# Graph attention on one core: one more gathered tile in 45 groups fetched row by row, from ScalarE's queue

## The chip, the cores and the metric

The kernel runs on one core of one Trainium2 chip. The metric is the device time of one launch in microseconds; of the kernel before, three runs were timed.

## The reference

The reference is a two-layer graph attention network over 3,125 nodes and 103,125 directed edges (self edges stand apart, one per node). Cut to what matters here, one layer is:

```python
xn = layernorm(x) * g + b
xp = xn + (xn @ Wpos + bpos + deg * Wdeg + bdeg)
q, k, v = xp @ Wq + bq, xp @ Wk + bk, xp @ Wv + bv      # 8 heads of 16
att = clip(sum(q[dst] * k[src], per head) / sqrt(16), -50, 50)
alpha = softmax of att over the edges of each dst
x = x + segment_sum(v[src] * alpha, dst) @ Wo + bo
x = x + gelu(layernorm(x) @ W1 + b1) @ W2 + b2
```

The edges are sorted by destination. `k[src]` and `v[src]` are rows of a table of 3,200 x 256 floats (1 KB a row) that the kernel writes to HBM once per layer; fetching the row of each edge's source is the gather that this case is about.

## The kernel before

**Tiles and groups.** The edges are cut into 806 tiles of 128; four tiles make a group, 202 groups a layer (the last one has two tiles). The first six groups are seams: tiles in which two destination blocks meet, which need two one-hot matrices. The edge loop runs over the groups of a layer, and each engine has its own copy of it, kept in step by semaphores.

**One group on each engine.** GpSimd gathers the group's rows of the table with one indirect DMA per tile (L857) into a ring of eight groups, `kvr`; before it starts group n it waits for `s_msg` of group n-8 (L854). ScalarE builds the transposed one-hot of group n+2 (`edge_spread`, L1327 to L1339: an Abs activation, L1335, and a Relu, L1339, both 128x512; a seam group has two such pairs), after the two Exp activations of group n (`edge_exp`, L1341 to L1348), which wait for VectorE. TensorE spreads the queries over the edges (L1135) and sums the messages per destination (L1148). VectorE multiplies keys and queries (`edge_prod`, L1728 to L1735), reduces, clips and guards them (L1740 to L1751), multiplies values by the weights (`edge_msg`, L1753 to L1761, which signals `s_msg`) and adds the sums to `agg` (L1769).

**Dense parts.** The 25 destination blocks are handled in nine chunks. As soon as a chunk's edges are summed, its dense parts (norm, attention output, two layer norms, Gelu, and in the first layer also the next layer's projections) are worked off in the slots of the edge loop that follow, at fixed offsets from the chunk's base slot: chunks 0 to 8 have their bases at slots 32, 56, 81, 105, 129, 154, 178, 195 and 203. On ScalarE (L1296 to L1325) a root stands at base+3 (L1172), Gelu at base+6 and base+7 (L1294, two activations each), and in the first layer a second root at base+10. Exp, Gelu and Sqrt need different activation tables, so that each of these slots has a table load before it and one back. The program order of ScalarE in a slot is `edge_exp(n)`, `edge_spread(n + 2)`, `dense_parts`.

**Rows fetched by SyncE.** In eight groups a layer, 25, 50, ..., 200 (`ROW_GROUPS`, L122), the group's last tile is not gathered by GpSimd. SyncE reads the source numbers of the tile into registers, six at a time (L748), and starts one DMA of 1 KB per row (L751), in the 22 slots that end four slots before the group. The rows land in `kv_rows`, which has two buffers; VectorE then takes this tile in an instruction of its own (L1734, L1758). The source numbers are loaded to one partition at the start (L672), ahead of the stores of the first layer's table (L681) on the same queue, for which GpSimd's first gather waits. SyncE also issues the loads of destination rows (`relT`, L664), the ordering of `q` and `x` by block (L688, L693), the second layer's table (L721) and the output.

Of the kernel before, what the change touches and what calls it, by code (L numbers as in the profile page):

```python
# [25 lines left out]
I32 = mybir.dt.int32  # L26
U32 = mybir.dt.uint32
U8 = mybir.dt.uint8
ALU = mybir.AluOpType
ACT = mybir.ActivationFunctionType  # L30
AX = mybir.AxisListType.X
ENG = mybir.EngineType

P = 128
N, D, H, L, FF = 3125, 128, 8, 2, 512
# [3 lines left out]
NP = BLOCKS * P  # L39
# [14 lines left out]
GROUPS = SEAM_GROUPS + MAIN_GROUPS  # L54
# [14 lines left out]
KV = 2 * D  # L69
# [12 lines left out]
NCH = len(CHUNKS)  # L82
# [30 lines left out]
KV_PAIRS = [(b, min(2, BLOCKS - b)) for b in range(0, BLOCKS, 2)]  # L113
# [8 lines left out]
ROW_GROUPS = [25 + 25 * i for i in range(8)]  # L122
# [2 lines left out]
ROW_TILE = G - 1  # L125


DVE_NORM, DVE_O, DVE_LN2, DVE_Y, DVE_LN1, DVE_QKV, DVE_SCORES, DVE_LOOP = 0, 2, 4, 9, 11, 13, 15, 17
PE_OUT, PE_O, PE_LN2, PE_FF, PE_Y, PE_LN1, PE_QKV = 1, 2, 5, 6, 8, 12, 13
ACT_OUT, ACT_STD2, ACT_LN2, ACT_FF, ACT_STD1, ACT_LN1, ACT_Q, ACT_LOOP = 1, 3, 5, 6, 10, 12, 15, 16  # L130
# [33 lines left out]
def step_of(n):  # L164

    return n // GROUPS, n % GROUPS
# [6 lines left out]

def by_rows(n):

    return n % GROUPS in ROW_GROUPS


def pool_gathers(n):
# [4 lines left out]
def row_turn(n):  # L184

    l, g = step_of(n)
    return l * len(ROW_GROUPS) + ROW_GROUPS.index(g)


def is_seam(n):  # L190
    return n % GROUPS < SEAM_GROUPS
# [102 lines left out]
def build(nc, x_in, src_flat, src_tiles, dst_tiles, dst_last, weights, out):  # L294
    with ExitStack() as ctx:
        def sb(name, shape, dt=F32):
            return ctx.enter_context(nc.sbuf_tensor(name, shape, dt))

        def sem(name):
            return ctx.enter_context(nc.semaphore(name))  # L300

        bank = [ctx.enter_context(nc.psum_tensor(f"bank{i}", [P, 512], F32)) for i in range(8)]

        kv_table = [nc.dram_tensor(f"kv_table{l}", [NP, KV], F32, kind="Internal").ap() for l in range(L)]
# [46 lines left out]
        apart = sb("apart", [P, G * P], BF16)  # L351
        kvr = sb("kvr", [P, RING, G, KV])
        kv_rows = sb("kv_rows", [P, 2, KV])
        row_src = sb("row_src", [1, len(ROW_GROUPS), P], I32)
        onehot = sb("onehot", [P, OH, G, P])
        onehotT = sb("onehotT", [P, OHT, G, P])
        prod = sb("prod", [P, G, D])
# [3 lines left out]
        msg = sb("msg", [P, 2, G, AGG])  # L361
# [6 lines left out]
        number = sb("number", [P, BLOCKS])  # L368
# [125 lines left out]
        s_first_table = sem("s_first_table")  # L494
# [24 lines left out]
        s_table = [sem(f"s_table{u}") for u in range(2)]  # L519
# [8 lines left out]
        s_apart = sem("s_apart")  # L528
        s_kv = [sem(f"s_kv{r}") for r in range(RING)]
        s_row_src = sem("s_row_src")  # L530
        s_kv_rows = [sem(f"s_kv_rows{u}") for u in range(2)]
        s_oh = sem("s_oh")
        s_ohT = sem("s_ohT")
# [7 lines left out]
        s_msg = sem("s_msg")  # L541
# [24 lines left out]
        def buffer(phase, c):  # L566

            return (phase * NCH + c) % 2

        def stored(phase, c):  # L570

            return 16 * sum(CHUNKS[k][1] for p in range(1, phase + 1) for k in range(NCH)
                            if buffer(p, k) == buffer(phase, c) and (p, k) <= (phase, c))
# [55 lines left out]
        def _(sp):  # L629
# [37 lines left out]
            rel_rows(1)  # L667

            sp.wait_ge(s_rows, 16 * 2 * SC)
            for i, g in enumerate(ROW_GROUPS):  # L670
                c, row = divmod(row_of(g, at_begin=True) + ROW_TILE, P)
                sp.dma_start(row_src[0:1, i, :], step_src[row:row + 1, c * P:(c + 1) * P]).then_inc(s_row_src, 16)  # L672

# [6 lines left out]
                    sp.wait_ge(*read(0, i, "kv"))  # L680
                sp.dma_start(table[:, b0:b0 + nb, :], kv_of(b0, nb)).then_inc(s_first_table, 16)  # L681

            sp.wait_ge(s_row_src, 16 * len(ROW_GROUPS))
            for c, (b0, nb) in enumerate(NAT):
                ranks = read_block_ranks(ENG.SP, b0, nb)
                sp.wait_ge(*read(0, c, "q"))
# [66 lines left out]
            for l in range(L):  # L753
                for s in range(SLOTS):
# [3 lines left out]
                    for i, g in enumerate(ROW_GROUPS):  # L758
                        part = s - (g - 3 - ROW_SLOTS)
# [409 lines left out]
        def _(act):  # L1169
# [157 lines left out]
            def edge_spread(n):  # L1327

                for h, m in enumerate(hots(n)):
                    r = 2 * h + n % GROUPS % 2 if is_seam(n) else m % BODY  # L1330
                    if m % BODY == 0:
                        act.wait_ge(s_relT[m // BODY % 2], 16 * (m // BODY // 2 + 1))
                    if m:
                        act.wait_ge(s_ohT, m)
                    act.activation(apart[:], relT[:, m // BODY % 2, r, :], ACT.Abs, bias=minus_p[:]).then_inc(s_apart, 1)  # L1335
                    act.wait_ge(s_apart, m + 1)
                    if m >= OHT:
                        act.wait_ge(s_qe, group_of(m - OHT) + 1)
                    act.activation(onehotT[:, m % OHT, :, :].rearrange("p j e -> p (j e)"), apart[:], ACT.Relu, bias=1.0, scale=-1.0).then_inc(s_ohT, 1)  # L1339

            def edge_exp(n):  # L1341

                act.wait_ge(s_attc, n + 1)
                t = gathers(n)
                act.activation(ex[:, 0:t * H], attc[:, n % 2, 0:t * H], ACT.Exp).then_inc(s_ex, 1)  # L1345
                if n >= 2:
                    act.wait_ge(s_agg_ps, n - 1)
                act.activation(msg[:, n % 2, 0:t, D:AGG], attc[:, n % 2, 0:t * H].rearrange("p (j h) -> p j h", h=H), ACT.Exp).then_inc(s_den, 1)  # L1348
# [5 lines left out]
            for l in range(L):  # L1354
                for s in range(SLOTS):
                    n = l * GROUPS + s
                    if s < GROUPS:
                        edge_exp(n)
                        if s + 2 < GROUPS:
                            edge_spread(n + 2)  # L1360
                    dense_parts(l + 1, s)
                    if l + 1 < L and s - BASE[-1] in ACT_NEXT:
                        edge_spread((l + 1) * GROUPS + ACT_NEXT.index(s - BASE[-1]))

        @program.vector
        def _(dve):
# [193 lines left out]
            def by_head(t):  # L1560
                return t.rearrange("p b (h d) -> p b h d", d=HD)
# [164 lines left out]
            def edge_prod(n):  # L1726

                dve.wait_ge(s_kv[n % RING], landed(n))  # L1728
                dve.wait_ge(s_qe, n + 1)
                t = pool_gathers(n)  # L1730
                if by_rows(n):
                    k = row_turn(n)
                    dve.wait_ge(s_kv_rows[k % 2], 16 * P * (k // 2 + 1))
                    dve.tensor_tensor(prod[:, t, :], kv_rows[:, k % 2, 0:D], bank[2][:, t * D:(t + 1) * D], ALU.mult)  # L1734
                dve.tensor_tensor(prod[:, 0:t, :], kvr[:, n % RING, 0:t, 0:D], bank[2][:, 0:t * D].rearrange("p (j c) -> p j c", c=D), ALU.mult).then_inc(s_prod, 1)  # L1735

            def edge_att(n):
# [15 lines left out]
            def edge_msg(n):  # L1753

                dve.wait_ge(s_ex, n + 1)
                t = pool_gathers(n)
                if by_rows(n):
                    dve.tensor_tensor(by_head(msg[:, n % 2, t:t + 1, 0:D]), by_head(kv_rows[:, row_turn(n) % 2:row_turn(n) % 2 + 1, D:KV]),  # L1758
                                      ex[:, t * H:(t + 1) * H].rearrange("p (j h) -> p j h", h=H).unsqueeze(3).broadcast_to([P, 1, H, HD]), ALU.mult)
                dve.tensor_tensor(by_head(msg[:, n % 2, 0:t, 0:D]), by_head(kvr[:, n % RING, 0:t, D:KV]),  # L1760
                                  ex[:, 0:t * H].rearrange("p (j h) -> p j h", h=H).unsqueeze(3).broadcast_to([P, t, H, HD]), ALU.mult).then_inc(s_msg, 1)  # L1761
# [68 lines left out]
            for l in range(L):  # L1830
                if l:
                    dve.wait_ge(s_agg0, l * NCH)
                for s in range(SLOTS):
                    n = l * GROUPS + s
# [54 lines left out]
```

## Time and profile before

| | us |
|---|---|
| median of 3 runs | 2166.88 |
| lowest, highest | 2166.07, 2170.96 |
| the profiled execution | 2163.2 |
| its span | 2161.5 |
| POOL (GpSimd) busy | 1552.6 (72%) |
| DVE (VectorE) busy | 1713.3 (79%) |
| PE (TensorE) busy | 1429.3 (66%) |
| ACT (ScalarE) busy | 940.6 (44%) |
| granted TensorE clock, mean | 0.804 of full speed |

How to read it: the span is the time from the first to the last instruction of one profiled execution, and the 1.7 us around it belong to that execution's own time. Busy time counts compute instructions and GpSimd's indirect DMAs; register instructions and the DMA issues of SyncE are not counted. In the rows, PE, DVE, ACT, POOL and SP are TensorE, VectorE, ScalarE, GpSimd and SyncE; a q behind the name means the engine's sequencer.

### The profile page before, as it was taken

How to read it: one execution, taken by the hardware profiler on the slowest of the kernel's cores; microseconds unless marked ns; L12 is line 12 of the kernel's file. 1: busy time of each engine (PE TensorE's matmuls, PEld its weight loads, DVE VectorE, ACT ScalarE, POOL GpSimd, SP SyncE). 2: the span in 40 equal slices, each digit the busy share in tenths (PEclk: the TensorE clock that was granted, in tenths of full speed). 3: DMA queues.
4: the chain of work that ended last, by engine and by line, in shares of the span. 5: the costliest groups of instructions: out<-in, count | busy, mean ns of one | idle time of the engine just before them, and what ended most of it. 6: DMA issues, size and time to landing. Idle time of an engine off the chain costs nothing.

```text
span 2161.5 us, 38930 instructions
## 1 busy us (share of the span) xinstructions
PE 1429.3 (66%) x8227; PEld 1248.0 (58%) x8227; DVE 1713.3 (79%) x5135; ACT 940.6 (44%) x2179; POOL 1552.6 (72%) x1653
## 2 busy tenths in 40 slices
PE   4866676776667666666777656566666767665666
PEld 4655565655556555555656556565565656555565
DVE  8759888889888878787877777787777778777876
ACT  8333354444535353534454335344343535344344
POOL 6177777777777777777727777777777777777773
PEclk9979878777977788887888778877886778788788
DMA  2365544454444444444424444444444444444441
GB/s 88 111 185 157 161 150 150 143 151 135 139 141 127 143 136 143 128 143 136 133 69 145 126 136 136 140 126 140 136 136 129 139 136 130 137 136 139 127 140 58
DMA packets 127140, 289.73 MB, mean 134 GB/s; under 512 B 33572, under 2 KB 61152, under 8 KB 126912
## 3 DMA queue, kind: packets, MB, share of 16 engines
q0 software_dynamic: 77056, 210.21, 33.8%
q1 hardware_dynamic: 49856, 77.03, 10.8%
q8 instruction: 76, 1.25, 0.2%
q14 instruction: 152, 1.25, 0.2%
HBM read 275.44 MB, written 8.38 MB: 131 GB/s over the span
## 4 chain that ended last, share of the span: by engine, by line
POOL 40%; issue 20%; DVE 14%; PE 13%; ACT 5%; DMA 4%; SPq 3%; DVEq 1%; ACTq 0%
POOL kvr L857 40%; PE bank L1135 5%; PE bank L1148 4%; DVE agg L1769 4%; DMA kvr<-kv_table,srcidx 3%; DVE kvr L1378 2%; DVE prod L1735 1%; ACT apart L1335 1%; ACT onehotT L1339 1%; SPq L751 1%; DVE onehot L1723 1%; PE bank L1092 1%; ACT L1294 1%; ACT L1345 1%; SPq L748 1%
## 5 line engine op out<-in xcount | busy, mean ns | idle before, releaser
L857 POOL DMA_INDIRECT kvr<-kv_table,srcidx x1596 | 1512.8, 948 | 543.8 <-issue 476.6
L1135 PE MATMUL bank<-q,onehotT 128*128 x3320 | 612.6, 342 | 683.9 <-DVE prod L1735 407.5
L1135 PEld LDWEIGHTS bank<-q,onehotT 128*128 128x128 f32 x3320 | 521.9, 240 | 796.3 <-issue 795.1
L1148 PE MATMUL bank<-msg,onehot 128*128 128x136 f32 x3320 | 615.0, 345 | 1.4 <-DVE msg L1760 1.2
L1148 PEld LDWEIGHTS bank<-msg,onehot 128*128 128x128 f32 x3320 | 574.8, 253 | 3.7 <-DVE msg L1760 3.5
L1345 ACT ACTIVATE bank<-attc 128x32 f32<-128x32 f32 x404 | 81.2, 201 | 1118.4 <-DVE attc L1751 1114.2
L1769 DVE TENSOR_TENSOR agg<-agg,bank 128x136 f32 x1624 | 470.7, 290 | 66.2 <-PE bank L1148 59.4
L1735 DVE TENSOR_TENSOR prod<-kvr,bank 128x512 f32<-128x512 f32 (+1 forms) x404 | 273.7, 678 | 232.2 <-DMA kvr<-kv_table,srcidx 190.9
L1335 ACT ACTIVATE apart<-relT,minus_p 128x512 bf16<-128x512 bf16 x416 | 293.8, 706 | 7.1 <-DMA relT<-rel_table 6.7
L1723 DVE TENSOR_TENSOR onehot<-bank,rel 128x512 f32<-128x512 f32 x416 | 282.8, 682 | 0.2
L1760 DVE TENSOR_TENSOR msg<-kvr,bank 128x512 f32<-128x512 f32 (+1 forms) x404 | 272.1, 674 | 12.2 <-ACT bank L1345 11.9
L1740 DVE TENSOR_REDUCE att<-prod 128x32 f32<-128x512 f32 x404 | 273.3, 677 | 0.1
L1339 ACT ACTIVATE onehotT<-apart 128x512 f32<-128x512 bf16 x416 | 261.9, 629 | 13.2
L1348 ACT ACTIVATE msg<-attc 128x32 f32<-128x32 f32 x404 | 86.0, 213 | 0.0
L1746 DVE TENSOR_SCALAR attc<-att 128x32 f32<-128x32 f32 x404 | 80.4, 199 | 0.0
L1751 DVE COPY_PREDICATED attc<-attnan,zeros 128x32 f32<-128x32 uint8 x404 | 76.8, 190 | 0.0
L1745 DVE TENSOR_TENSOR attnan<-att 128x32 uint8<-128x32 f32 x404 | 74.8, 185 | 0.1
L1604 DVE TENSOR_TENSOR x<-x,bank 128x384 f32<-128x384 f32 (+1 forms) x36 | 18.9, 524 | 68.6 <-PE bank L1092 38.9
L1345 ACT ACT_TABLE_LOAD x51 | 65.4, 1283 | 0.9
L1092 PE MATMUL bank<-w,hT 128*128 128x128 f32 x400 | 59.4, 293 | 0.0
L1378 DVE TENSOR_TENSOR kvr<-kvr,q 128x3328 bf16<-128x3328 bf16 (+1 forms) x32 | 55.0, 1772 | 2.5 <-PE bank L884 2.4
L1079 PE MATMUL bank<-xnT,w 128*128 128x384 f32 (+1 forms) x144 | 55.4, 516 | 0.7 <-ACT xnT L1272 0.7
(219 smaller groups left out, 857.6 us busy)
## 6 DMA issues: line engine op xcount, KB each, us to landing
relT<-rel_table SPq DMA_DIRECT2D x104, 512.0 KB
kv_rows<-kv_table SPq DMA_DIRECT2D x2048, 1.0 KB
kvr<-kv_table,srcidx POOLq DMA_INDIRECT x1596
loop_kv<-kv_table SPq DMA_DIRECT2D x25, 128.0 KB, 2.8
kv_table<-qkv SPq DMA_DIRECT2D x25, 128.0 KB, 2.5
kv_table<-onehot SPq DMA_DIRECT2D x8, 256.0 KB, 2.2
w<-weights SPq DMA_DIRECT2D x2, 840.0 KB, 7.3
loops<-x_in SPq DMA_DIRECT2D x5, 320.0 KB, 5.4
```

The lines of the kernel that those rows point to most:

```text
L857: pool.indirect_dma_start(kvr[:, n % RING, j, :], None, kv_table[l], bass.IndirectOffsetOnAxis(ap=srcidx[:, step:step + 1], axis=0)).then_ ...
L1135: mm = pe.matmul(bank[2][:, j * D:(j + 1) * D], onehotT[:, m % OHT, j, :], q[:, bass.ds(ranks[j + h], 1), :].rearrange("p a c -> p (a c)") ...
L1148: mm = pe.matmul(sum_ps(n, k), onehot[:, m % OH, j, :], msg[:, n % 2, j, :], start=(m, j) == of[0], stop=(m, j) == of[-1])
L1335: act.activation(apart[:], relT[:, m // BODY % 2, r, :], ACT.Abs, bias=minus_p[:]).then_inc(s_apart, 1)
L1339: act.activation(onehotT[:, m % OHT, :, :].rearrange("p j e -> p (j e)"), apart[:], ACT.Relu, bias=1.0, scale=-1.0).then_inc(s_ohT, 1)
L1345: act.activation(ex[:, 0:t * H], attc[:, n % 2, 0:t * H], ACT.Exp).then_inc(s_ex, 1)
L1378: return dve.tensor_tensor(oh[:, k % 2, :, :, :], digit[:, 0:count_of, :].unsqueeze(1).broadcast_to(shape), of_step.unsqueeze(2).broadcast ...
L1723: dve.tensor_tensor(onehot[:, m % OH, :, :], iota_ps.unsqueeze(1).broadcast_to([P, G, P]), rel[:, row:row + G].unsqueeze(2).broadcast_to([ ...
L1735: dve.tensor_tensor(prod[:, 0:t, :], kvr[:, n % RING, 0:t, 0:D], bank[2][:, 0:t * D].rearrange("p (j c) -> p j c", c=D), ALU.mult).then_in ...
L1740: dve.tensor_reduce(att[:, n % 2, 0:t * H], prod[:, 0:t, :].rearrange("p j (h d) -> p (j h) d", d=HD), AX, ALU.add).then_inc(s_att, 1)
L1760: dve.tensor_tensor(by_head(msg[:, n % 2, 0:t, 0:D]), by_head(kvr[:, n % RING, 0:t, D:KV]), ex[:, 0:t * H].rearrange("p (j h) -> p j h", h ...
L1769: dve.tensor_tensor(target, target, sum_ps(n, j), ALU.add).then_inc(s_agg, 1)
```

## The change

Four more groups a layer, 46, 91, 136 and 181 (`ACT_ROW_GROUPS`), have their last tile fetched row by row. ScalarE does this: three rows a slot, right behind `edge_spread` and ahead of the dense parts, in the 43 slots that end four slots before the group. Each slot holds one register load of three values and three DMAs with a register address (the last one two). The rows have a buffer pair and semaphores of their own. SyncE loads four more rows of source numbers at the start. GpSimd gathers three tiles instead of four in these groups, and VectorE takes the fourth from the new buffers. The diff, cut to its core:

```diff
+ACT_ROW_GROUPS = [46 + 45 * i for i in range(4)]
+ACT_ROWS_A_SLOT = 3
+ACT_ROW_SLOTS = -(-P // ACT_ROWS_A_SLOT)
...
 def by_rows(n):
-    return n % GROUPS in ROW_GROUPS
+    return n % GROUPS in ROW_GROUPS + ACT_ROW_GROUPS
...
-            for i, g in enumerate(ROW_GROUPS):
+            for i, g in enumerate(ROW_GROUPS + ACT_ROW_GROUPS):
                 c, row = divmod(row_of(g, at_begin=True) + ROW_TILE, P)
                 sp.dma_start(row_src[0:1, i, :], step_src[row:row + 1, c * P:(c + 1) * P]).then_inc(s_row_src, 16)
...
+            def fetch_rows(l, i, part):                      # ScalarE
+                k = l * len(ACT_ROW_GROUPS) + i
+                if part == 0:
+                    if k == 0:
+                        act.wait_ge(s_row_src, 16 * len(ROW_GROUPS + ACT_ROW_GROUPS))
+                    if i == 0 and l == 0:
+                        act.wait_ge(s_first_table, 16 * len(KV_PAIRS))
+                    elif i == 0:
+                        for u in range(2):
+                            c = NCH - 1 - u
+                            act.wait_ge(s_table[buffer(l, c)], stored(l, c))
+                    if k >= 2:
+                        act.wait_ge(s_msg, (k - 2) // len(ACT_ROW_GROUPS) * GROUPS + ACT_ROW_GROUPS[(k - 2) % len(ACT_ROW_GROUPS)] + 1)
+                p0, p1 = part * ACT_ROWS_A_SLOT, min(P, (part + 1) * ACT_ROWS_A_SLOT)
+                nodes = nc.values_load_multi_w_load_instructions(row_src[0:1, len(ROW_GROUPS) + i, p0:p1], engines=(ENG.Activation,), min_val=0, max_val=NP - 1,
+                                                                 skip_runtime_bounds_check_because="the number of a node")[1]
+                for p, node in zip(range(p0, p1), nodes):
+                    act.dma_start(act_kv_rows[p:p + 1, k % 2, :], kv_table[l][bass.ds(node, 1), :]).then_inc(s_act_kv_rows[k % 2], 16)
...
                         edge_exp(n)
                         if s + 2 < GROUPS:
                             edge_spread(n + 2)
+                        for i, g in enumerate(ACT_ROW_GROUPS):
+                            part = s - (g - 3 - ACT_ROW_SLOTS)
+                            if 0 <= part < ACT_ROW_SLOTS:
+                                fetch_rows(l, i, part)
                     dense_parts(l + 1, s)
...
                 if by_rows(n):                               # VectorE, edge_prod; edge_msg alike
                     k = row_turn(n)
-                    dve.wait_ge(s_kv_rows[k % 2], 16 * P * (k // 2 + 1))
-                    dve.tensor_tensor(prod[:, t, :], kv_rows[:, k % 2, 0:D], bank[2][:, t * D:(t + 1) * D], ALU.mult)
+                    landed_rows, rows = (s_act_kv_rows, act_kv_rows) if n % GROUPS in ACT_ROW_GROUPS else (s_kv_rows, kv_rows)
+                    dve.wait_ge(landed_rows[k % 2], 16 * P * (k // 2 + 1))
+                    dve.tensor_tensor(prod[:, t, :], rows[:, k % 2, 0:D], bank[2][:, t * D:(t + 1) * D], ALU.mult)
```

## Rows read from the trace of the kernel before

**Rows 1.** The page, the chain that ended last, by engine

```profile
POOL 40%; issue 20%; DVE 14%; PE 13%; ACT 5%; DMA 4%; SPq 3%; DVEq 1%; ACTq 0%
```

**Rows 2.** Waits of POOL, whole run: us in total, times, longest us

```profile
POOL kvr L857 <- issue: 476.6, 1564, 0.3
POOL kvr L857 <- DMA kv_table<-qkv: 35.0, 1, 35.0
...
POOL kvr L857 <- DVE msg L1760: 9.1, 30, 0.3
```

**Rows 3.** Timeline, DVE and POOL: start us, us, engine, line, operation, tiles

```profile
153.20 0.68 DVE L1760 TENSOR_TENSOR msg<-kvr,bank 128x512 f32<-128x512 f32 x1
154.42 0.95 POOL L857 DMA_INDIRECT kvr<-kv_table,srcidx  x1 [0.30 <-issue]
...
481.27 0.68 DVE L1760 TENSOR_TENSOR msg<-kvr,bank 128x512 f32<-128x512 f32 x1
...
496.97 0.95 POOL L857 DMA_INDIRECT kvr<-kv_table,srcidx  x1 [0.30 <-issue]
```

**Rows 4.** Waits of DVE for gathers: whole run, then 607 to 1136, 1136 to 2162

```profile
DVE prod L1735 <- DMA kvr<-kv_table,srcidx: 190.9, 144, 3.9
...
DVE prod L1735 <- DMA kvr<-kv_table,srcidx: 36.1, 26, 3.4
...
DVE prod L1735 <- DMA kvr<-kv_table,srcidx: 154.8, 118, 3.9
```

**Rows 5.** SP's row DMAs and a three-value load (ns min/median/max), and a timeline row

```profile
L751 SPq DMA_DIRECT2D kv_rows<-kv_table x2048: 224/228/344, 139.2 to 2110.7; - x187
...
L623 SPq TENSOR_LOAD <-permrow x27: 280/928/947, 228.2 to 2147.0; - x27
...
241.92 2.32 SPq L751 DMA_DIRECT2D kv_rows<-kv_table  x6
```

**Rows 6.** DVE's register load, 704 to 705 us, and the timeline of DVE there

```profile
L618 DVEq TENSOR_LOAD <-rankrow x1: 342/342/342, 704.7 to 704.7; - x1
...
704.69 0.61 DVE L1623 SCALAR_TENSOR_TENSOR qkv<-u_deg,deg,bank 128x384 f32<-128x384 f32 x1 [0.52 <-PE bank L1046]
```

**Rows 7.** Timeline of ACT, a quick plain slot

```profile
168.91 0.20 ACT L1345 ACTIVATE bank<-attc 128x32 f32<-128x32 f32 x1 [2.36 <-DVE attc L1751]
...
169.90 0.63 ACT L1339 ACTIVATE onehotT<-apart 128x512 f32<-128x512 bf16 x1
172.45 0.20 ACT L1345 ACTIVATE bank<-attc 128x32 f32<-128x32 f32 x1 [1.92 <-DVE attc L1751]
```

**Rows 8.** Timeline of ACT and DVE, chunk 0: second Gelu slot, first root, second root

```profile
311.27 0.20 ACT L1345 ACTIVATE bank<-attc 128x32 f32<-128x32 f32 x1 [0.33 <-DVE attc L1751]
...
312.26 0.63 ACT L1339 ACTIVATE onehotT<-apart 128x512 f32<-128x512 bf16 x1
312.91 1.28 ACT L1294 ACT_TABLE_LOAD   x1
...
316.57 0.20 ACT L1345 ACTIVATE bank<-attc 128x32 f32<-128x32 f32 x1
...
316.80 0.69 DVE L1760 TENSOR_TENSOR msg<-kvr,bank 128x512 f32<-128x512 f32 x1
...
294.80 0.30 ACT L1172 ACTIVATE std<-mv,eps 128x3 f32<-128x3 f32 x1
...
296.11 0.17 DVE L1580 RECIPROCAL rstd<-std 128x3 f32<-128x3 f32 x1
...
330.08 0.30 ACT L1172 ACTIVATE std<-mv,eps 128x3 f32<-128x3 f32 x1
...
330.56 0.17 DVE L1580 RECIPROCAL rstd<-std 128x3 f32<-128x3 f32 x1
```

**Rows 9.** SP at the start: timeline row, and its waits

```profile
77.73 5.41 SPq L672 DMA_DIRECT2D row_src<-q  x8
...
SPq L681 <- DVE kvr L1537: 5.0, 4, 1.3
```

More of the change, by code:

```diff
@@ L186, in row_turn @@
     l, g = step_of(n)
-    return l * len(ROW_GROUPS) + ROW_GROUPS.index(g)
+    groups = ROW_GROUPS if g in ROW_GROUPS else ACT_ROW_GROUPS
+    return l * len(groups) + groups.index(g)
 def is_seam(n):
@@ L353, in build @@
         kv_rows = sb("kv_rows", [P, 2, KV])
-        row_src = sb("row_src", [1, len(ROW_GROUPS), P], I32)
+        row_src = sb("row_src", [1, len(ROW_GROUPS) + len(ACT_ROW_GROUPS), P], I32)
+        act_kv_rows = sb("act_kv_rows", [P, 2, KV])
         onehot = sb("onehot", [P, OH, G, P])
@@ L530, in build @@
         s_row_src = sem("s_row_src")
+        s_act_kv_rows = [sem(f"s_act_kv_rows{u}") for u in range(2)]
         s_kv_rows = [sem(f"s_kv_rows{u}") for u in range(2)]
@@ L681, in _ @@
                 sp.dma_start(table[:, b0:b0 + nb, :], kv_of(b0, nb)).then_inc(s_first_table, 16)
-            sp.wait_ge(s_row_src, 16 * len(ROW_GROUPS))
+            sp.wait_ge(s_row_src, 16 * len(ROW_GROUPS + ACT_ROW_GROUPS))
             for c, (b0, nb) in enumerate(NAT):
@@ L1757, in edge_msg @@
                 if by_rows(n):
-                    dve.tensor_tensor(by_head(msg[:, n % 2, t:t + 1, 0:D]), by_head(kv_rows[:, row_turn(n) % 2:row_turn(n) % 2 + 1, D:KV]),
+                    rows = act_kv_rows if n % GROUPS in ACT_ROW_GROUPS else kv_rows
+                    dve.tensor_tensor(by_head(msg[:, n % 2, t:t + 1, 0:D]), by_head(rows[:, row_turn(n) % 2:row_turn(n) % 2 + 1, D:KV]),
                                       ex[:, t * H:(t + 1) * H].rearrange("p (j h) -> p j h", h=H).unsqueeze(3).broadcast_to([P, 1, H, HD]), ALU.mult)
```

## Prediction

> **What bounds the kernel now.** I read the page's chain first. Six tenths of the chain that ended last are GpSimd's gathers with the issue gaps between them [rows 1]. One gather takes 0.95 us and the next starts 0.30 us later, so the cadence is 1.25 us [rows 3]. The waits of GpSimd come next [rows 2]: 1,564 of its 1,596 idle gaps before a gather are this issue gap, at most 0.3 us long. Besides them it waited 35.0 us for the second layer's table, and the 30 waits put down to VectorE's message together make 9.1 us, 0.3 us each, which is the issue gap again. So GpSimd runs without a stop inside both layers, and 1,596 x 1.25 = 1,995 us of the 2,161.5 us span are its cadence.
>
> Two reserves decide whether a shorter gather stream shows. **The ring**: gathers of group n wait for the message of group n-8. The message of group 3 ends at 153.20+0.68 = 153.88, and group 11's first gather starts at 154.42: 0.54 us to spare. At group 80 it is 496.97 against 481.95: 15.0 us [rows 3]. **VectorE's slack**: it waited for gathered rows 190.9 us in the whole run, 36.1 us between 607 and 1136 us, 154.8 us after 1136 us [rows 4]. 36.1+154.8 = 190.9, so up to 607 us it never waited for a gather. The first layer has 36.1 us of slack, all of it in its second half, and the second layer has 154.8.
>
> **The change part by part.**
>
> *Removed:* one gather in groups 46, 91, 136 and 181 of each layer: 8 x 1.25 = 10.0 us, 5.0 per layer, on the engine that paces both.
>
> *SyncE's four more loads of source numbers.* Eight took 5.41 us, so four take 2.7 [rows 9]. They stand ahead of the stores of the first table, for which GpSimd waits. But SyncE stood idle among these stores for VectorE, 5.0 us in one group of waits [rows 9], more than 2.7. Nothing; without that cover, 2.7 us at the start.
>
> *VectorE:* in eight more groups its products and messages fall into two instructions. No row for this is needed: two extra instructions in 8 groups are some us spread over both layers, inside the slack above. The wait on the rows' semaphore stands in front of the product; the last rows are issued four slots ahead, some 20 us, against landings of a few us, so I cost it at nothing.
>
> *ScalarE's issue, per slot.* The trace has no DMA that ScalarE issues; the nearest rows are SyncE's of the same kind. Six rows took 2.32 us from the first issue to the end of the last, one issue 0.228 us: (2.32-0.23)/5 = 0.41 us a row with its address arithmetic. A register load of three values took 0.93 us (median) [rows 5]. So a slot costs C = 0.93+3x0.41 = 2.2 us of ScalarE's sequencer, in 43 slots per tile, 344 in all. Lower bound: 0, should its sequencer work ahead. Upper bound: no cheaper row excludes a dearer issue; a one-partition row on SyncE went up to 0.34 us, and if each row took 0.23 us more (it always meets one of SyncE's), C = 2.9. I take 2.2, since it is the same transfer, and load, on another sequencer.
>
> *When does it start?* VectorE's sequencer began its register load at 704.7, when the compute instruction ahead of it started (704.69), after that one had waited 0.52 us, and not while it was still waiting [rows 6]. I let ScalarE's load begin with the start of the second one-hot activation (L1339). The Trainium skill (Perfetto Trace Analysis, "DVE / Act Engine Instruction") has the sequencer free for the next instruction once the compute instruction is pushed into a wait queue. By that rule the issue would lie wholly in ScalarE's wait for VectorE, and the sum would be the removed 10.0 us alone; the row above speaks against it.
>
> *Plain slots.* The one-hot activation starts 1.0 us after the slot's Exp (168.91, 169.90), so the engine is free again at 1.0+2.2 = 3.2 us; the next Exp came after 3.54 us in the quickest stretches [rows 7], after 5 us at GpSimd's pace. Hidden, with 0.36 us left. The cover is ScalarE's wait for VectorE.
>
> *Slots with a table load.* The rows stand between the one-hot and the dense parts. The table load for Gelu started 0.65 us after the start of the one-hot (312.26, 312.91); now it starts 2.2 us after it: pushed by 1.53 us. In two Gelu slots in a row the pushes add up, less the 0.33 us that ScalarE idled between them: Exp of group 40 moves from 316.57 by 2x1.53-0.33 = 2.7 us, and VectorE's message at 316.80 waits for it [rows 8]. A root moves by 1.53 too: VectorE's reciprocal (L1580) follows at 296.11 where the root ends at 295.10, so it loses 1.53-1.01 = 0.5; the other one, 330.56 against 330.38, loses 1.4 [rows 8]. By the slots of the kernel, six chunks of a layer fall under these fetches: five Gelu pairs, one single Gelu slot (88 has no rows), six first roots and, in the first layer, six second roots. First layer: 5x2.7+1.5+6x0.5+6x1.4 = 26.4 us. Second layer: 18.0 us. If each of the 23 slots of the first layer cost its whole push: 35 us.
>
> *Where it goes.* Second layer: 18+5 is far below 154.8: the 5.0 us are kept. First layer: 26.4+5.0 = 31.4 against 36.1: kept, with 4.7 to spare; the part up to 607 us (three chunks, some 13 us) must fit the ring, which has 15.0 at group 80 with two chunks' 10 us behind it. At group 11 there are only 0.54 us; should the push of one slot (1.53) reach group 3's message whole, GpSimd loses 1.0 us there. I cost it at nothing and leave the 1.0 to the margin below, since a slot there has two one-hot pairs and a long wait behind them.
>
> **The sum.** -10.0, plus 1.5 as a margin for the start (1.0) and for a first layer that comes this close to its limit (0.5, my choice): -8.5 us. The profiled execution took 2,163.2 us (span 2,161.5), 0.17% below the median of the three runs, 2,166.9; the same 8.5 us taken from the median give 2,158.4.
>
> **The rivals.**
>
> (a) *The first layer's gain is lost, about even.* Formula for the first layer: its end moves by X-36.1, but not below -5.0, where X is what the stages lose. With X = 36 to 41 the layer gives between 0 and +5 and the whole -5 to 0: around 2,164.4. For it: the last wait for gathers of this layer lies well before its end, VectorE's own work sets the last groups, and 26.4 is close. Against it: the count of full pushes gives 35 only if nothing absorbs any. Chance 0.2.
>
> (b) *ScalarE's issue is dear: slower.* Above C = 2.54 (3.54-1.0) the quickest plain slots are stretched too; I count 25 of under 3.6 us in the first 104 groups, where VectorE is catching up. Then X = 26.4x(C-0.64)/1.53 + 25x(C-2.54). At C = 2.9: 39+9 = 48, the layer ends 12 us later, the second gains 5: +7, 2,174. At 3.4: 48+21 = 69, +33-5 = +28, 2,195. It decides from X = 41.1, which is C = 2.7, or 0.6 us a row. For it: no row shows ScalarE issuing. Against it: SyncE's issue stayed between 0.224 and 0.344 us in all 2,048 rows [rows 5]. The Trainium skill (Perfetto Trace Analysis, "DMA Instruction — HWDGE") has the descriptor generator locked for one sequencer at a time; by that rule rows of both engines wait for each other. No run here shows two engines at it. Chance 0.17.
>
> (c) *Nothing arrives:* the gather stream is not shortened, since GpSimd takes longer over the groups around (the ring closes for as long as is saved), 2,166.9. For it the 0.54 us at group 11; against it 15 us at group 80. That GpSimd still fetches the tile is excluded: its count of gathers comes from the same test (by_rows) as the new fetch. Chance 0.05.
>
> **How the numbers follow.** A measurement of this kernel can tell some 0.2%, 4.3 us, from no change. Forecast 2,158.4, chance 0.58, its own range 2,156 to 2,161. Rival (a) from 2,162 to 2,167: a quarter of it still faster by over 0.2%. So faster 0.63, same 0.2, slower 0.17. The range runs from 2,155.5 (all ten, and a run at the low end) to 2,170, which takes in (a) and the near part of (b).
>
> **What would show it.** GpSimd x1588 gathers, the cadence still 1.25 us, and no wait for VectorE's message over 0.3 us; ScalarE's load at about 0.9 us and rows 0.41 us apart, from the start of L1339; the Gelu table load 2.2 us after it; VectorE's waits for gathers down by some 20 to 31 us in the first layer and by about 23 in the second; the second layer's first gather about 5 us earlier. Wrong if a row costs over 0.5 us on ScalarE, if VectorE's wait for gathers in the first layer falls to near zero, or if GpSimd's wait between the layers grows beyond 36 us: then the saving was there and was handed back.

## The result, and the profile after

| | before | changed |
|---|---|---|
| median, us | 2165.98 (9 runs) | 2171.74 (9 runs) |
| lowest, highest | 2164.02, 2170.96 | 2169.03, 2177.05 |
| the profiled execution, its span | 2163.2, 2161.5 | 2175.1, 2173.4 |

The ratio is 1.0031, 95% interval 1.0023 to 1.0040: the change makes the kernel 0.3%, some 6 us, slower. I had forecast 8.5 us faster. The profiled execution of before is shorter than all nine timed runs, that of the changed kernel is its second longest: the spans lie 12 us apart where the medians lie 6, and what is read from the two traces below holds for these two executions.

The page's chain that ended last, by engine, for the changed kernel; ScalarE has gone from 5% to 11% [rows 1], and its sequencer (ACTq) from nothing to 2%:

```profile
POOL 24%; DVE 19%; issue 19%; PE 17%; ACT 11%; SPq 3%; DMA 3%; ACTq 2%; DVEq 2%
```

The waits of POOL, whole run (us in total, times, longest us), which answer to [rows 2]:

```profile
POOL kvr L865 <- issue: 472.4, 1550, 0.3
POOL kvr L865 <- DMA kv_table<-qkv: 50.1, 1, 50.1
...
POOL kvr L865 <- DVE msg L1794: 16.2, 36, 2.3
```

The first layer's saving was handed back: the wait for the second layer's table is 15.1 us longer, and six waits for VectorE's message, up to 2.3 us, show that the ring closed six times between 603 and 855 us. They make 7.1 us. The first of them, and the first gather of each layer, in the timeline of POOL:

```profile
98.82 0.99 POOL L865 DMA_INDIRECT kvr<-kv_table,srcidx  x1 [21.33 <-DMA kv_table<-xn]
...
603.63 0.94 POOL L865 DMA_INDIRECT kvr<-kv_table,srcidx  x1 [0.92 <-DVE msg L1794]
...
1149.52 0.94 POOL L865 DMA_INDIRECT kvr<-kv_table,srcidx  x1 [50.07 <-DMA kv_table<-qkv]
```

The same two gathers in the kernel before:

```profile
99.36 0.99 POOL L857 DMA_INDIRECT kvr<-kv_table,srcidx  x1 [23.11 <-DMA kv_table<-xn]
...
1133.82 0.94 POOL L857 DMA_INDIRECT kvr<-kv_table,srcidx  x1 [34.99 <-DMA kv_table<-qkv]
```

From the first layer's first gather to the second's it is now 1,050.7 us. Before it was 1,034.5: the first layer takes 16.2 us more. From there to the end it is 1,023.9 against 1,027.7: the second gives 3.8. Sum 12.4, less 0.5 for an earlier start, is the 11.9 between the two spans.

VectorE's largest waits from 607 to 1136 us:

```profile
DVE agg L1803 <- PE bank L1156: 18.7, 27, 1.2
DVE msg L1794 <- ACT bank L1373: 16.3, 8, 2.9
DVE x L1636 <- PE bank L1079: 15.2, 6, 4.1
DVE qkv L1655 <- PE bank L1054: 11.7, 12, 2.1
DVE x L1636 <- PE bank L1100: 9.1, 4, 2.9
DVE rstd L1612 <- ACT std L1180: 5.3, 6, 1.4
```

In this window of before its 36.1 us for gathers stood on top [rows 4]. Of its other waits there these count below, for the products of TensorE that the dense parts add (L1092, L1071, L1046) and for ScalarE's Exp:

```profile
DVE x L1604 <- PE bank L1092: 13.2, 5, 5.0
...
DVE x L1604 <- PE bank L1071: 10.2, 6, 3.0
DVE qkv L1623 <- PE bank L1046: 9.1, 12, 2.2
...
DVE msg L1760 <- ACT bank L1345: 2.1, 3, 1.4
```

No wait for gathers is left in the first layer; those of the second, 154.8 us before, are these:

```profile
DVE prod L1768 <- DMA kvr<-kv_table,srcidx: 119.7, 89, 3.9
```

ScalarE's issue, by line (ns min/median/max), which answers to [rows 5]:

```profile
L1364 ACTq TENSOR_LOAD <-row_src x344: 656/878/1467, 130.5 to 2034.9; - x172
...
L1367 ACTq DMA_DIRECT2D act_kv_rows<-kv_table x1024: 213/213/520, 131.6 to 2036.3; - x171
```

And the timeline of ACT in the first of the two Gelu slots of chunk 0 ([rows 8] has the second one of before). The rows end 2.2 us after the start of L1347, and only then does the table load start:

```profile
308.15 0.20 ACT L1373 ACTIVATE bank<-attc 128x32 f32<-128x32 f32 x1 [1.00 <-DVE attc L1784]
...
309.14 0.63 ACT L1347 ACTIVATE onehotT<-apart 128x512 f32<-128x512 bf16 x1
310.18 1.19 ACTq L1367 DMA_DIRECT2D act_kv_rows<-kv_table  x3
311.39 1.28 ACT L1302 ACT_TABLE_LOAD   x1 [1.62 <-issue]
...
315.18 0.18 ACT L1373 ACTIVATE bank<-attc 128x32 f32<-128x32 f32 x1
```

### The profile page after: what moved, and what is told of

It is laid out like the page before. It is cut to its first block, busy times and chain, and to the rows that moved or that the text cites. A ratio compares the mean times of both kernels' runs of the same rounds, so it can differ in the third digit from the quotient of the medians.

```text
span 2173.4 us, 42362 instructions
## 1 busy us (share of the span) xinstructions
PE 1423.7 (66%) x8227; PEld 1240.1 (57%) x8227; DVE 1712.4 (79%) x5151; ACT 943.8 (43%) x2179; POOL 1546.2 (71%) x1645
## 3 DMA queue, kind: packets, MB, share of 16 engines
q10 hardware_dynamic: 2048, 1.05, 0.2%
## 4 chain that ended last, share of the span: by engine, by line
POOL 24%; DVE 19%; issue 19%; PE 17%; ACT 11%; SPq 3%; DMA 3%; ACTq 2%; DVEq 2%
POOL kvr L865 24%; DVE agg L1803 6%; PE bank L1143 6%; PE bank L1156 5%; ACT apart L1343 2%; ACT onehotT L1347 2%; DVE kvr L1410 2%; DVE prod L1768 2%; ACTq L1367 2%; DMA kvr<-kv_table,srcidx 2%; PE bank L1100 2%; ACT L1373 1%; DVE onehot L1755 1%; ACT L1302 1%; SPq L759 1%
## 5 line engine op out<-in xcount | busy, mean ns | idle before, releaser
L1143 PE MATMUL bank<-q,onehotT 128*128 x3320 | 606.0, 339 | 678.3 <-ACT onehotT L1347 364.2
L1156 PE MATMUL bank<-msg,onehot 128*128 128x136 f32 x3320 | 603.7, 341 | 1.3 <-DVE msg L1794 1.3
L1156 PEld LDWEIGHTS bank<-msg,onehot 128*128 128x128 f32 x3320 | 563.2, 248 | 3.5 <-DVE msg L1794 3.2
L1768 DVE TENSOR_TENSOR prod<-kvr,bank 128x512 f32<-128x512 f32 (+1 forms) x404 | 272.2, 674 | 166.2 <-DMA kvr<-kv_table,srcidx 119.7
L1347 ACT ACTIVATE onehotT<-apart 128x512 f32<-128x512 bf16 x416 | 261.9, 630 | 13.1
L1100 PE MATMUL bank<-w,hT 128*128 128x128 f32 x400 | 66.1, 315 | 0.0
L1100 PEld LDWEIGHTS bank<-w,hT 128*128 128x128 f32 x400 | 55.7, 215 | 3.9
```

What stands on the lines that cost most here:

```text
L1100: mm = pe.matmul(o, hT[:, f, j * P:(j + 1) * P], w[l][:, W_2 + f * D:W_2 + (f + 1) * D], start=False, stop=f == FC - 1)
L1143: mm = pe.matmul(bank[2][:, j * D:(j + 1) * D], onehotT[:, m % OHT, j, :], q[:, bass.ds(ranks[j + h], 1), :].rearrange("p a c -> p (a c)") ...
L1156: mm = pe.matmul(sum_ps(n, k), onehot[:, m % OH, j, :], msg[:, n % 2, j, :], start=(m, j) == of[0], stop=(m, j) == of[-1])
```

## The experiments

Below, "slots" are counted from a chunk's base, as in the text above. Each version was timed beside the kernel before, on the same chip. The ratio and, in brackets, its 95% interval come from these runs together and differ a little from the quotient of the two medians.

To compare first layers I use one number for each run, **X = 36.1 + s - w**: what VectorE's stages lose in the first layer. s is how much longer than 1,034.5 us it takes from the first gather to the second layer's first, and w is what VectorE still waits for gathers between 607 and 1136 us (the undivided product's line alone, as in [rows 4]). If its stages take X longer, that first uses up what it waits for gathers, and what remains moves the layer's end. The changed kernel has s = 16.2, w = 0, X = 52. Two runs in which nothing is laid on ScalarE in this layer show the scatter of X: -6 (the first run below) and 5 (the last of the third group). So two values of X less than some 10 us apart are not told apart.

The layers of before that I compare with are quick ones. Five other first layers that keep all their gathers and have an X of 3 or less took 1,035.1 to 1,039.1 us, and second layers that no run touched took 1,027.2 to 1,031.0: s can overstate a loss by up to 4.6 us.

### Which layer loses, and does the issue alone do it?

The second layer only (in the first layer no rows, all gathers). Here `act_slots(l, i)` lists the slots of tile i in layer l: the same 43 as in the change, and none in a layer that is not in `ACT_ISSUED`. Cut to its core:

```diff
+ACT_USED = (1,)
+ACT_ISSUED = (1,)
...
-    return n % GROUPS in ROW_GROUPS + ACT_ROW_GROUPS
+    return n % GROUPS in ROW_GROUPS or act_rows(n)
+
+
+def act_rows(n):
+
+    return n % GROUPS in ACT_ROW_GROUPS and n // GROUPS in ACT_USED
...
-                            part = s - (g - 3 - ACT_ROW_SLOTS)
-                            if 0 <= part < ACT_ROW_SLOTS:
-                                fetch_rows(l, i, part)
+                            if s in act_slots(l, i):
+                                fetch_rows(l, i, act_slots(l, i).index(s))
```

> Rows by ScalarE in the second layer only; in the first GpSimd gathers all tiles and ScalarE issues nothing. Theory (first layer loses because ScalarE's issue, 2.2 us a slot, makes its dense parts late and VectorE's 36.1 us of slack is less than that): the first layer is as before, GpSimd's wait for the second table back at about 35 us, the second layer keeps its 5.0 us: 2161 us, 0.23% below before. Rival (the loss is in the rows themselves, in either layer, or in SyncE's longer start): no gain, 2166 or more.

Measured: 2160.12 us, ratio 0.9977 (0.9966 to 0.9987); the second layer takes 1,024.0 us, 3.7 less than before, the first has X = -6, and the table wait is 37.6. The loss is the first layer's.

The first layer's issue alone: `ACT_USED = ()` and `ACT_ISSUED = (0,)`, so that GpSimd gathers everything and the rows land in a buffer that nobody reads. As no reader holds the buffers back, ScalarE waits at the start of a tile until the rows of the tile two before have landed.

> ScalarE loads registers and starts all 512 row DMAs of the first layer, in the same slots, but GpSimd gathers every tile of both layers and VectorE's instructions are those of before: the cost of the issue alone. Theory (stages lose about 52 us against 36.1 us of slack): the first layer ends 15 to 16 us later whether its four gathers are there or not, since VectorE sets it: 2181 us; VectorE's wait for gathers between 607 and 1136 us zero, GpSimd's wait for the second table 50 us. Rival 1 (my forecast's 26.4 us was right and something else, VectorE's divided instructions or the closing ring, makes the loss): 2166 us with some 10 us of VectorE's 36.1 left. Rival 2 (ScalarE's stages are innocent, the rows' DMAs hold up GpSimd's gathers): a gather takes longer than 0.95 us.

Measured: 2177.02 us, ratio 1.0046 (1.0033 to 1.0059). Its wait of POOL for the table:

```profile
POOL kvr L893 <- DMA kv_table<-qkv: 42.3, 1, 42.3
```

And VectorE's waits from 607 to 1136 us:

```profile
DVE agg L1838 <- PE bank L1184: 20.4, 29, 1.2
DVE msg L1829 <- ACT bank L1406: 19.6, 9, 2.9
...
DVE rstd L1647 <- ACT std L1208: 5.4, 7, 1.4
```

No wait for gathers is left though all gathers are made: s = 11.3, X = 47. A gather still takes 0.94 to 0.95 us, so the rows' DMAs don't hold GpSimd up. The issue on ScalarE is the cause; VectorE's divided instructions and the missing gathers are not needed for it. Nor is the ring: behind 155 us no wait of GpSimd for VectorE's message is over 0.3 us in this run. It lost 11, not the 15 to 16 that I expected; the 5 us to the changed kernel lie within the scatter of X.

### Which part of the issue, in which slots?

As the run above, with a `return` ahead of the row DMAs, and without the waits for their landing:

> As the one before, with the register load of three values in each slot but no row DMA: the issue per slot is 0.9 us in place of 2.2. Theory (X grows with what the issue pushes beyond the 0.65 us that lay between the one-hot's start and the next activation): a push of 0.25 us instead of 1.5 a stage, X some 5 to 9 us, the layer ends as before, 2166 us, VectorE's wait for gathers in the first layer 27 to 31 us. Rival (waiting on the loaded registers is what costs, not the rows): near 0 us of wait left and 2175 or more.

Measured: 2169.52 us (one run; before 2165.89), w = 39.2, s = 3.6, X = 0.5. The load alone takes nothing of VectorE's slack. Both layers of this execution were 3 to 4 us longer than those of before, the second one too, in which nothing was changed.

As the issue alone, but with rows in chosen slots only (`if s in act_slots(l, i)`, a list of slots by their distance from the last base):

> Cost of the issue alone again, first layer, rows only in the 100 slots that lie more than 12 slots behind a chunk's base, so none in a slot with a dense part on ScalarE but the projections'. Theory (plain slots hide 2.2 us): X under 5 us, VectorE's wait for gathers in the first layer 31 to 36 us, 2166 us. Rival (plain slots, stretched where VectorE catches up, carry a good part of the 52 us): under 20 us of wait left, and a table wait of over 35 us on GpSimd.

> Cost of the issue alone, first layer, rows only in the 12 slots with Gelu (base+6, base+7). Forecast's count of these: 5 pairs x 2.7 + 1.5 = 15 us, so 21 us of VectorE's 36.1 us wait for gathers left. Theory (a push in a Gelu slot is paid twice: by the next Exp, and two slots on where x += y waits for TensorE's product of the late Gelu): 12 x 1.53 x 1.3 to 2 = 24 to 37 us, 0 to 12 us of wait left; the layer ends as before or up to 3 us later.

> Cost of the issue alone, first layer, rows only in the 24 slots base+1, +2, +3 and +5: the copies ahead of the attention output, the first root and the copy ahead of the Gelu. Forecast's count: only the six roots, 3 us in all, so 33 us of wait left. Theory (each of these copies stands between VectorE and TensorE, a push of 1.5 us comes through to x += o and to the norm): 8 to 16 us, 20 to 28 us of wait left. Both with no change of the end, 2166 us.

| rows in | slots | us (one run; before 2165.89, 2164.89, 2164.89) | s | w | X |
|---|---|---|---|---|---|
| plain slots (over 12 behind a base) | 100 | 2164.20 | 0.7 | 33.5 | 3 |
| Gelu slots (base+6, +7) | 12 | 2165.47 | 4.5 | 2.5 | 38 |
| copies and first root (base+1, 2, 3, 5) | 24 | 2166.54 | 3.6 | 38.8 | 1 |

Plain slots hide 2.2 us, as forecast. Twelve slots with Gelu, 36 rows, nearly use up VectorE's slack on their own (the changed kernel has rows in eleven of them, not in slot 88). For the copy slots I expected 8 to 16 us by my new theory, and the forecast's 3 was nearer. VectorE's waits of the Gelu run in the window:

```profile
DVE msg L1829 <- ACT bank L1406: 17.2, 8, 2.9
DVE x L1671 <- PE bank L1107: 17.1, 6, 3.9
DVE x L1671 <- PE bank L1128: 15.7, 6, 4.8
DVE qkv L1690 <- PE bank L1082: 15.4, 12, 3.2
...
DVE prod L1803 <- DMA kvr<-kv_table,srcidx: 2.5, 3, 1.1
```

The late Exp takes 17.2 us, 15.1 more than before. The three waits for TensorE below it make 48.2 against 10.2+13.2+9.1 = 32.5 before, 15.7 more, though two of them stand in slots that hold no rows here. So of the 33.6 us of waits for gathers that are gone in this window, Exp takes somewhat less than half, and TensorE as much again. I read the longer waits for TensorE as ones that a wait for gathers in the same groups used to cover; no run tests that by itself. Up to 607 us VectorE's waits for Exp grow as well, from 4.9 to 13.4 us: over the whole layer the late Exp takes 23.6 us of the 38. One of the eight waits for Exp, in the timeline of ACT and DVE of this run:

```profile
787.41 0.20 ACT L1406 ACTIVATE bank<-attc 128x32 f32<-128x32 f32 x1 [1.36 <-DVE attc L1819]
...
789.50 1.19 ACTq L1399 DMA_DIRECT2D act_kv_rows<-kv_table  x3
...
790.78 1.28 ACT L1330 ACT_TABLE_LOAD   x1 [1.74 <-DMA act_kv_rows<-kv_table]
...
794.43 0.20 ACT L1406 ACTIVATE bank<-attc 128x32 f32<-128x32 f32 x1
...
794.67 0.69 DVE L1829 TENSOR_TENSOR msg<-kvr,bank 128x512 f32<-128x512 f32 x1 [2.95 <-ACT bank L1406]
```

From Exp to Exp it is 7.02 us in this slot where a Gelu slot of the kernel before takes 5.30 (786.31 to 791.61 in its trace, group 136), and a plain one 3.54 in a quick stretch [rows 7]. All twelve take 6.9 to 7.2 us here and 5.3 to 6.0 before, 18.7 us more together.

### Fewer slots, chosen slots, and the removed term by itself

Four rows a slot in 32 slots a tile (`ACT_ROWS_A_SLOT = 4`), and the same without rows in base+6 and base+7:

> The change with four rows a slot in place of three, in 32 slots a tile in place of 43: 256 slots in all instead of 344, rows and groups the same. Theory (the loss goes with the number of dense slots that hold rows times the issue's length): the register load of four takes 0.3 to 0.4 us in place of 0.88, so a slot costs about 0.35+0.45+3x0.37 = 1.9 us and a push is 1.25; X falls from 52 by the 25% fewer slots and the 18% shorter push to some 32 to 38 us: 2157 to 2162 us. Rival (what counts is the number of rows, 1,024 at 0.37 us or more): as the change, 2171 us.

> The kernel with four rows a slot, whose rows now keep out of the slots base+6 and base+7 (Gelu) in both layers; still 32 slots a tile, the same eight gathers removed. Theory (Gelu slots carry two thirds of the first layer's loss, 33.6 us of VectorE's waits for gathers in the run that had rows there alone): the rest of X is 10 to 15 us against 36.1, the first layer keeps its 5.0 us: 2156 to 2157 us, and VectorE waits for gathers 15 us or more in the first layer. Rival (the roots and copies would carry it in their place, being pushed in any case): 2162 us as with Gelu.

Measured: 2162.75 us, ratio 0.9986 (0.9975 to 0.9996), X = 41; and 2156.31 us, ratio 0.9958 (0.9944 to 0.9971), w = 8.1, s = -2.7, X = 25. Both theories on the first run are too plain: X fell by 11 us, but only to 41. Without Gelu slots the first layer is 2.7 us shorter than before, of 5.0 removed, yet 25 us of X remain, more than the copies' run led me to expect; its second layer took 1,027.4 us in the profiled execution, no less than before. The parts don't add up slot by slot: the Gelu slots cost 38 us by themselves, but keeping rows out of them saved 16 here; what the second root (base+10) and the slots behind the Gelu carry wasn't run by itself.

Two versions with other tiles, four rows a slot: six in the second layer (36 + 33 i, all slots), and two or three in the first, in slots free of dense work.

> Four rows a slot; in the second layer six tiles (groups 36, 69, ..., 201) in all slots, in the first two tiles (groups 36 and 135) in slots more than 12 behind a chunk's base only. GpSimd is rid of 8 gathers as in the change, 2 and 6. Theory: the first layer loses nothing and gives 2.5 us, the second gives 7.5 of which about 1 is lost: 2157 us, faster than both kernels. Rival (the second layer's slack runs out near its end, or four rows stretch plain slots): 2162 to 2166 us.

> As the version with 2 and 6 tiles, but three tiles in the first layer (groups 36, 102, 168), in slots that lie outside base+1, 2, 3, 5, 6, 7, 8, 9 and 10. Nine gathers less in all: 11.3 us. Theory: the first layer loses nothing and gives 3.75 us, the second 7.5 less about 1: 2154.5 us. Rival (three tiles close the ring early, or the slots at base+4, 11 and 12 carry a loss): 2156 us or more.

Measured: 2155.47 us, ratio 0.9960 (0.9947 to 0.9974), w = 30.3; and 2154.55 us, ratio 0.9952 (0.9938 to 0.9965), w = 29.7. Both first layers have X = 6, at the edge of the scatter, for 2 and 3 tiles. In both, the tile of group 201, which has two tiles only, gets another tile's rows in the second layer.

The gathers left out, with nothing in their place:

```diff
-    return 16 * sum(pool_gathers(k) for k
+    return 16 * sum(pool_gathers(k) - left_out(k) for k
...
-                for j in range(pool_gathers(n)):
+                for j in range(pool_gathers(n) - left_out(n)):
```

> The kernel before, in which GpSimd leaves out the last tile's gather of groups 46, 91, 136 and 181 of each layer; VectorE reads what the ring held eight groups earlier, so these eight tiles' rows are those of other edges. It is the removed term by itself: no rows, no issue on ScalarE. Theory: 8 x 1.25 = 10.0 us all arrive, 2156 us, VectorE's wait for gathers in the first layer 31 us, GpSimd's table wait 35 us. Rival (the first layer is not GpSimd's to shorten, since 12 of the 36.1 us of waits lie in slots where ScalarE's Gelu is right behind): 5 us, 2161, and the table wait 40 us.

Measured: 2158.24 us, ratio 0.9967 (0.9954 to 0.9980), w = 30.8, table wait 37.3: 7.1 us by the ratio (4.3 to 10.0). GpSimd waited once for VectorE's message for 2.7 us, at 157 us. That is group 11, with its 0.54 us to spare [rows 3], and comes long ahead of group 46, the first gather left out, so it belongs to this execution and not to what was removed. The 10.0 us are the end of the interval: most of the removed term arrives, all of it perhaps.

### The place of the rows in ScalarE's program

The change, with its rows behind the dense parts:

```diff
-                        for i, g in enumerate(ACT_ROW_GROUPS):
-                            part = s - (g - 3 - ACT_ROW_SLOTS)
-                            if 0 <= part < ACT_ROW_SLOTS:
-                                fetch_rows(l, i, part)
                     dense_parts(l + 1, s)
+                    for i, g in enumerate(ACT_ROW_GROUPS):
+                        part = s - (g - 3 - ACT_ROW_SLOTS)
+                        if 0 <= part < ACT_ROW_SLOTS:
+                            fetch_rows(l, i, part)
```

> The change with its three rows a slot behind the dense parts in place of ahead of them. Roots, copies and Gelu are no longer pushed, only the next group's Exp, where ScalarE is late. Theory (in a Gelu slot ScalarE is the limit whatever the order, 5.3 us from Exp to Exp without rows and 7.0 with them against VectorE's 3.5): Gelu slots cost what they cost in the change, only the roots' and copies' 10 to 15 us fall away: 2160 to 2166 us. Rival (the loss comes by late Gelu, copies and roots, not by the late Exp): nothing left of it, 2157 us.

Measured: 2157.57 us, ratio 0.9965 (0.9952 to 0.9979), w = 32.6, s = -1.9, X = 2. My theory fell, the rival's number came out: all of the loss is gone with the order of two calls. VectorE's largest wait in the window is for gathers again:

```profile
DVE prod L1768 <- DMA kvr<-kv_table,srcidx: 32.6, 23, 2.9
```

ACT and its queue in the second Gelu slot of chunk 0, in the timeline:

```profile
312.60 0.20 ACT L1373 ACTIVATE bank<-attc 128x32 f32<-128x32 f32 x1
...
313.59 0.63 ACT L1347 ACTIVATE onehotT<-apart 128x512 f32<-128x512 bf16 x1
314.24 1.28 ACT L1302 ACT_TABLE_LOAD   x1
314.64 0.82 ACTq L1367 DMA_DIRECT2D act_kv_rows<-kv_table  x2
315.53 0.58 ACT L1302 ACTIVATE hT<-bank,w 128x384 f32<-128x384 f32 x1
315.61 0.21 ACTq L1367 DMA_DIRECT2D act_kv_rows<-kv_table  x1
316.01 0.57 ACT L1302 ACTIVATE hT<-bank,w 128x384 f32<-128x384 f32 x1
316.60 1.28 ACT L1373 ACT_TABLE_LOAD   x1
317.89 0.20 ACT L1373 ACTIVATE bank<-attc 128x32 f32<-128x32 f32 x1
```

Three rows are issued *before* the second Gelu activation runs, though they stand behind it in the program. The register load starts at 313.6 in this slot, the start of L1347: the sequencer had handed over the table load and both Gelu activations by then and went on to the rows. So the slot stays 5.29 us long, and the issue lies beside the table load. In all twelve Gelu slots of the chunks 0 to 5 the table load starts 0.65 us after L1347 again, as before the change. In the change's order, ahead of the dense parts, the same 2.2 us keep the table load itself from being handed over.

The issue alone in this place:

> Cost of the issue alone, first layer, all 43 slots a tile, GpSimd gathering every tile, as in the second experiment, but with the rows behind the dense parts. Theory (ScalarE's sequencer goes on past the queued table load and Gelu and issues the rows while they run, so a Gelu slot stays 5.3 us from Exp to Exp): VectorE's wait for gathers in the first layer stays at 30 to 37 us, GpSimd's table wait at 35 us, 2166 us. Rival (the version behind the dense parts still lost some and only shifted it to where the trace shows none): under 25 us of wait left, or 2168 us and more.

Measured: 2170.17 us, and before 2169.47 on the same chip, ratio 1.0000 (0.9990 to 1.0010), w = 39.3, table wait 35.6. 512 rows and 172 loads cost nothing there, within 0.1%, against 1.0046 in the change's place: the gain of the version before this one does not cover up a cost.

Then more of it: four rows a slot, six tiles in both layers, behind the dense parts; first at 36 + 33 i, then at 35 + 32 i, which leaves group 201 alone.

> Rows behind the dense parts, four a slot, six tiles (groups 36, 69, ..., 201) in both layers: 12 gathers less, 15.0 us. Theory (the issue is hidden in nearly every slot and VectorE's waits for gathers cover the rest): each layer gives 7.5 us less 1: 2151 to 2153 us, the fastest so far; VectorE's wait for gathers in the first layer 25 us or more. Rival (in the first layer the 12 us of waits in Gelu slots are none to draw on, VectorE sets the end, GpSimd's table wait grows by what is saved there): 2156 us, table wait 40 us.

> As the version with six tiles and four rows a slot behind the dense parts, but at groups 35, 67, ..., 195: group 201 has only two tiles, and the version before this one (as those with tiles at 36 + 33 i in the second layer) put another tile's rows into its second. 12 gathers less, 15.0 us. Theory: as that version, 0.994 of before, a little below 2155 us where before takes 2166; VectorE's wait for gathers in the first layer about 27 us, GpSimd's table wait 35 to 37 us. Rival (a part of that version's gain came from the tile it did not fetch rightly): 0.996 or more.

Measured: ratio 0.9940 (0.9926 to 0.9953; 2157.59 against 2169.47), with another tile's rows in the second tile of group 201 in both layers, w = 26.9 and a table wait of 35.9; and 2151.92 us against 2164.29, ratio 0.9942 (0.9929 to 0.9956). The second is the fastest version that computes every edge: 12.4 us less than before, of 15.0 removed. Its VectorE still waits for gathers in the window,

```profile
DVE prod L1799 <- DMA kvr<-kv_table,srcidx: 31.5, 23, 4.0
```

and its GpSimd waits for the second table as before:

```profile
POOL kvr L893 <- DMA kv_table<-qkv: 35.5, 1, 35.5
```

## Why the prediction was wrong

**Right: the removed term.** 1,588 gathers at 948 ns, and the second layer gave 3.7 to 3.8 us of its 5.0, alone or with the first, against the one trace of before. The gathers left out gave 7.1 of 10.0, with the 10.0 at the end of the interval.

**Right: C.** The load took 0.88 us (forecast 0.93), a row 0.37 us from issue to issue (0.41), the first one of a slot longer (below); from the start of L1347 to the end of the last row it is 2.2 us, and in the change's order the load began with that start. Rival (b), a dear issue, is out: it was the only one that had the kernel slower, so the sign of the result came by a path to which I had given no slower time. That the two queues wait for each other was its ground in the Trainium skill (Perfetto Trace Analysis, "DMA Instruction — HWDGE"); 213 ns as median of 1,024 rows, beside SyncE's 2,048, does not show it: 396 of them overlap in time with an issue of SyncE's rows, and the median of these is 214 ns.

**Right: SyncE's loads, the plain slots.** The first gather started at 98.8 us (99.4 before), and 100 plain slots cost X = 3.

**Wrong: the term X of the first layer.** It was "5x2.7+1.5+6x0.5+6x1.4 = 26.4 us" and came to 52 in the changed kernel, 47 with the issue alone. Table loads were pushed by 1.6 to 1.7 us (1.1 in slot 87, which has two rows), with Exp, VectorE's message and the reciprocal late behind them, as the prediction has it; what the pushes cost VectorE was mis-sized by a factor of two. Clearest is this in the Gelu slots: I took 15 us for eleven of them, and twelve measured 38 by themselves. The 2.7 was read off chunk 0, the one place that I followed, and there it holds: 11.16 us from Exp to Exp two slots on (305.41 to 316.57) are now 14.1 in the Gelu run. But the late Exp alone took 23.6 us over the layer, and the waits for TensorE came on top, 15.7 us behind 607 us, for which the sum had no term. Why they grow was not tested; my reading is that an engine whose slack is gone pays in full what the slack had covered. Nor does all of the excess sit in the Gelu slots: with four rows a slot the version without them still had X = 25 where 3+8.4 = 11.4 us of the sum were left. The "upper bound" of 35 counted one push per slot and had no room for any of this, so it bounded nothing. The second layer points the same way: its waits for gathers fell from 154.8 to 119.7 us while it became 3.8 shorter, which makes 31 us lost where I had 18.0 (32 in the run with the second layer only; in the runs that put no rows ahead of this layer's dense parts the number lies between -18 and 8). There the slack hid it.

With w = 0 VectorE sets the end of the first layer, which is rival (a)'s mechanism. I had it stop at X = 41, about even; it came at some 1.3 times that.

**Wrong: the ring takes it up.** At group 97 VectorE's product started some 18 us later than before, the 15.0 us at group 80 had shrunk to 2.7, and the ring closed from 603 us on, as rival (c) has it for its own reason. It is not what made the loss: with the issue alone it stayed open, and the layer took 11.3 us more.

**Half right: the sequencer.** The Trainium skill (Perfetto Trace Analysis, "DVE / Act Engine Instruction") has it free once an instruction is pushed. In the change's order the trace speaks against it: the load waited for the start of L1347, in 342 of its 344 slots to within 7 ns. With the rows behind the dense parts it bears the page out: the sequencer went on past a queued table load and two activations. I had read the rule as one on whether the issue is hidden at all; here it decided what may stand ahead of it.

## What to carry to other kernels

Try work of an engine's sequencer (register loads, row DMAs) *behind* the compute instructions of its slot, not ahead: in this kernel what had been handed over ran beside the issue, and what stood behind the issue waited for it. One slot's push, priced in one place, isn't an upper bound of the slack that it uses up: other waits of the late engine grew here too, so compare its whole list of waits, not one. And test a cost by itself (the issue without the saving) before judging a saving: here the same 1,024 rows and eight gathers less are worth +0.3% or -0.35% by the rows' place alone.

## What the hardware showed that I had not expected

- The first row of a slot takes 0.45 us to issue on ScalarE, the next two 0.21 (in the slots of chunk 0), at an equal 1 KB each.
- A register load of four values took less time on ScalarE than one of three: 0.48 us (median of 256, in the version with four rows a slot) against 0.88 (median of 344, in the changed kernel). I had counted on 0.3 to 0.4 for four.
- The sequencer's lead is not fixed: in the version with the rows behind the dense parts the load started with L1347 in the slot shown, but in the Gelu slot before it only at 309.9, with the start of the Gelu activation. Whether a wait for TensorE held it there wasn't tried.
